# A decoder kernel on one core: a memory layer's centred values made by GpSimd in place of TensorE, with another order of work

## What is computed

```python
x = _layernorm(x + _L1_xattn_ref(x, ctx_1024, ctx_1024, ...), axis=-1)
...
Ctilde = jnp.einsum('bhid,bhjd->bhij', qh, kh) * D / TAU
maxit = jnp.maximum(jnp.abs(jnp.sum(Ctilde, axis=-1, keepdims=True)), jnp.exp(-max_d))
Htilde = jnp.einsum('bhij,bhjd->bhid', Ctilde, vh) / (maxit + 1e-06)
...
mean = jnp.mean(x, axis=-1, keepdims=True)
var = jnp.var(x, axis=-1, keepdims=True)
xn = (x - mean) / jnp.sqrt(var + 1e-05)
```

## Time and profile before

| what | value |
|---|---|
| median of three runs | 808.02 us (807.7 to 809.53) |
| profiled execution, span from first to last instruction | 808.1 us |
| its own time outside the span | not given by the page |
| PE busy | 738.1 us (91%) |
| PE weight loads busy | 485.7 us (60%) |
| DVE busy | 560.4 us (69%) |
| ACT busy | 347.2 us (43%) |
| POOL busy | 166.7 us (21%) |
| mean granted TensorE clock | 0.976 of full |

### The profile page before, as it was taken

The page is one execution under the profiler, slowest core; times in us unless marked ns, Lnnn a source line. Parts: engine busy times, 40 slices in busy tenths (PEclk is TensorE's granted clock), DMA queues, the critical chain, the costliest instruction groups (busy, mean ns, idle before and its releaser), DMA issues.

```text
span 808.1 us, 14850 instructions
## 1 busy us (share of the span) xinstructions
PE 738.1 (91%) x5976; PEld 485.7 (60%) x5976; DVE 560.4 (69%) x1405; ACT 347.2 (43%) x640; POOL 166.7 (21%) x249
## 2 busy tenths in 40 slices
PE   9999999989999978689979999999999998978494
PEld 6776565667657745557744576867656676646242
DVE  1558436575457589997899973647546569799887
ACT  3576223333144335565337634242324433485253
POOL 8711003010015030022330020011012513103300
PEclk9999999999999999999999999999999999988698
DMA  9402000000002000032000020000000000000001
GB/s 352 183 12 119 1 1 1 1 2 3 27 1 53 2 27 2 0 106 79 27 0 1 1 78 28 2 1 3 0 2 1 1 2 2 1 1 1 1 1 52
DMA packets 12739, 23.76 MB, mean 29 GB/s; under 512 B 768, under 2 KB 7040, under 8 KB 12416
## 3 DMA queue, kind: packets, MB, share of 16 engines
q1 hardware_dynamic: 12672, 22.82, 8.2%
HBM read 20.72 MB, written 2.10 MB: 28 GB/s over the span
## 4 chain that ended last, share of the span: by engine, by line
PE 73%; DVE 17%; ACT 4%; issue 2%; POOL 2%; DVEq 0%; ACTq 0%; POOLq 0%
PE bank L754 14%; PE bank L572 7%; PE bank L564 5%; PE bank L598 5%; PE bank L619 4%; PE bank L852 4%; PE bank L1104 3%; PE bank L764 3%; PE bank L740 3%; PE bank L833 2%; DVE work L1771 2%; PE bank L799 2%; PE bank L702 2%; PE bank L557 1%; PE bank L875 1%
## 5 line engine op out<-in xcount | busy, mean ns | idle before, releaser
L2160 POOL TENSOR_TENSOR rstd<-rstd,minus_half 128x2 f32<-128x2 f32 x56 | 43.1, 771 | 467.8 <-DVE rstd L1201 467.6
L754 PE MATMUL bank<-work,f0w 128*128 128x512 f16 x512 | 114.0, 379 | 0.0
L754 PEld LDWEIGHTS bank<-work,f0w 128*128 128x128 f16 x512 | 49.7, 98 | 59.5 <-issue 1.9
L1937 ACT ACTIVATE work<-bank 128x512 f16<-128x512 f32 x64 | 37.0, 596 | 83.7 <-PE bank L754 70.9
L1411 DVE SCALAR_TENSOR_TENSOR work<-bank,work 128x512 f16<-128x512 f32 x64 | 42.3, 685 | 35.3 <-ACT work L1937 35.2
L619 PE MATMUL bank<-work 128*128 128x256 f32 x208 | 50.2, 383 | 0.7 <-DVE work L1308 0.7
L1975 ACT ACTIVATE work<-bank 128x512 f32<-128x512 f32 x32 | 19.1, 596 | 72.6 <-PE bank L852 72.5
L1276 DVE TENSOR_REDUCE small<-bank 128x1 f32<-128x512 f32 (+3 forms) x32 | 18.8, 588 | 41.8 <-PE bank L600 41.7
L619 PEld LDWEIGHTS bank<-work 128*128 128x128 f32 x208 | 37.6, 190 | 6.8 <-issue 1.2
L1494 DVE TENSOR_TENSOR work<-bank,upper 128x512 f32<-128x512 f32 x32 | 22.0, 688 | 24.4 <-PE bank L852 24.3
L852 PE MATMUL bank<-work 64*128 64x128 f32 x512 | 37.2, 285 | 0.2 <-DVE work L1494 0.2
(11 more groups left out here) (307 smaller groups left out, 1698.1 us busy)
## 6 DMA issues: line engine op xcount, KB each, us to landing
work<-in_mask SPq DMA_DIRECT2D x4, 1024.0 KB, 7.0
xT<-in_xT SPq DMA_DIRECT2D x4, 512.0 KB, 4.0
ctxT<-in_ctxT SPq DMA_DIRECT2D x4, 512.0 KB, 4.7
perf_w<-in_k SPq DMA_DIRECT2D x3, 512.0 KB, 11.7
perf_w<-in_perf_w SPq DMA_DIRECT2D x1, 1536.0 KB, 6.2
x<-in_x SPq DMA_DIRECT2D x2, 512.0 KB, 11.7
ctx<-in_w SPq DMA_DIRECT2D x2, 512.0 KB, 13.8
work<-in_w SPq DMA_DIRECT2D x1, 1024.0 KB, 16.1
```

What stands on the lines that cost most here:

```text
L754: ins = nc.tensor.matmul(u.bank[:, :], f0w1[:, k, m * P:(m + 1) * P], s.h1[part][:, k, :], start=(k == 0 and part == 0), stop=(k == NF - 1 ...
L1937: nc.scalar.activation(dst[0][:, m, :], u.bank[:, :], ACT.Relu).then_inc(s.high_made.sem, 1)
L2160: nc.gpsimd.tensor_tensor(s.rstd[:, two], s.rstd[:, two], minus_half[:, 0:2], ALU.pow).then_inc(s.rstd_made.sem, 1)
```

## The change

The step mlstm.values goes from PE's and ACT's programs, and with it the matrix `centring`, its instruction on DVE, two bank uses per stream and round, and POOL's step mlstm.xT0. In its place POOL has a step mlstm.centre per stream and round, which reads the context in place, sums each head's 32 channels by halving adds in `s.l_v1`, scales by -1/32 and adds the mean to the context into `s.l_v1`. It stands in the front half: after the rstds of the cross step in round 1, after those of the sign step in round 0. `s.l_v1` moves to the end of the work region, which attention, sign and performer don't use.

```diff
@@ stream
-        s.l_v1 = w.cut(NT, LH, LV1)
...
+        w.at = w.words - NT * LH * LV1
+        s.l_v1 = w.cut(NT, LH, LV1)
@@ tensor_engine, back_half
-                if p == 0:
-                    yield "mlstm.values"
-
-                    if n == 0:
-                        pe.wait_ge(*centring_made.at(0))
-                    for i in range(2):
-                        u = s.banks["mlstm", n, "values", i]
-                        pe.wait_ge(*u.free)
-                        for j in range(2):
-                            t = 2 * i + j
-                            for k in range(NC):
-                                ins = nc.tensor.matmul(u.bank[:, j * C + k * P:j * C + (k + 1) * P], s.ctxT[:, k, t * P:(t + 1) * P],
-                                                       centring[:, :], start=True, stop=True)
-                        ins.then_inc(u.filled, 1)
@@ tensor_engine, the steps mlstm.state and mlstm.outT
-                    pe.wait_ge(*s.memory_ones.at(n))
-                    for i in range(2):
-                        pe.wait_ge(*s.banks["mlstm", n, "values", i].read)
+                    pe.wait_ge(*s.values_centred.at(n))
@@ vector_engine, prep
-            nc.vector.scalar_tensor_tensor(out=centring[:, :].rearrange("p (h d) -> p h d", d=LD), in0=mlstm_block[:, :, 0:LD],
...
@@ scalar_engine, back_half
-            yield "mlstm.values"
-            act.wait_ge(*s.memory_ones.at(n))
-            for i in range(2):
-                u = s.banks["mlstm", n, "values", i]
-                act.wait_ge(*u.full)
-                nc.scalar.copy(s.l_v1[:, 2 * i:2 * i + 2, :, 0:LD].rearrange("p t h d -> p (t h) d"),
-                               u.bank[:, :].rearrange("p (g d) -> p g d", d=LD)).then_inc(u.emptied, 1)
@@ gpsimd_engine
+        def centre(s, n):
+
+            yield "mlstm.centre"
+            pool.wait_ge(*s.ctx_in.all(n))
+            means, by_head = s.den2, ctx_of(s, n)[:, :, :].rearrange("p t (h d) -> p (t h) d", d=LD)
+            values = s.l_v1[:, :, :, :].rearrange("p t h d -> p (t h) d")
+            nc.gpsimd.memset(values[:, :, LD:LV1], 1.0)
+            half, src = LD // 2, by_head
+            while half >= 1:
+                out = values if half > 1 else means.unsqueeze(2)
+                m = gps.mark(nc.gpsimd.tensor_tensor(out[:, :, 0:half], src[:, :, 0:half], src[:, :, half:2 * half], ALU.add))
+                pool.wait_ge(*m)
+                half, src = half // 2, out
+            m = gps.mark(nc.gpsimd.tensor_scalar(means, means, -1.0 / LD, None, ALU.mult))
+            pool.wait_ge(*m)
+            nc.gpsimd.tensor_tensor(values[:, :, 0:LD], by_head,
+                                    means.unsqueeze(2).broadcast_to([P, NT * LH, LD]), ALU.add).then_inc(s.values_centred.sem, 1)
+
@@ gpsimd_engine, front_half
+            if n > 0:
+                yield from centre(s, n)
             for p in range(2):
                 yield from rstd(s, n, 3, p, "sign.")
+            if n == 0:
+                yield from centre(s, n)
@@ gpsimd_engine, back_half
-            yield "mlstm.xT0"
-            for p in range(2):
-                pool.wait_ge(*s.banks["perf", n, "out", p].full)
-            nc.gpsimd.memset(s.l_v1[:, :, :, LD:LV1], 1.0).then_inc(s.memory_ones.sem, 1)
```

More of the change, by code:

```diff
@@ L37 @@
     "tensor":
[8 rows of a table removed]
-    "vector":
[10 rows of a table removed]
-    "scalar":
[7 rows of a table removed]
[8 rows of a table added]
+    "vector":
[11 rows of a table added]
+    "scalar":
[7 rows of a table added]
     "gpsimd":
-        "a7 b2 a5 b5 a5 b2 a1 b3 a4 b1 a1 b4 a2 b1 a2 b1 a1 b2 a2 b1 a2 b1 a4 b2 a1 b2 a1 b5 a4 b4 w1 b1 a1 b1 a5 b10 a2 "
-        "b2",
+        "a7 b2 a2 b1 a3 b3 a1 b1 a5 b3 a4 b2 a1 b3 a1 b1 a1 b2 a2 b3 a1 b1 a4 b1 a2 b1 a1 b1 a1 b1 a1 b1 a1 b1 a1 b5 "
+        "a2 b1 a1 b1 a1 b2 w1 b1 a4 b1 a1 b9 a2 b2",
     "sync":
-        "w1 a2 w1 a1 w3 b1 w2 b1 a1 b1 w1 b1 a5 b1 a1 b1 a1 b6 a2 b1",
+        "w2 a1 w3 b1 a1 w1 b2 a1 b1 a1 w2 b1 a7 b7 a2 b1",
 }
 KEEP = {
[8 rows of a table removed]
[11 rows of a table added]
 }
@@ L236, in build @@
     mlstm_block = sb("mlstm_block", [P, LHT, LV1])
-    centring = sb("centring", [P, P])
     memory_back = sb("memory_back", [P, LHT, LV1])
@@ L361, in stream @@
         s.used, s.den_inverse = signal("masked_scores_used", NC * 2), signal("denominators_inverted", NC)
-        s.memory_ones, s.gate_low, s.softplus_made = (signal(name, 1) for name in ("memory_ones", "log_gate_in", "softplus"))
+        s.values_centred, s.gate_low, s.softplus_made = (signal(name, 1) for name in ("values_centred", "log_gate_in", "softplus"))
         s.key_gates, s.gates_final = (signal(name, 1) for name in ("key_gates_negated", "largest_gates_negated"))
@@ L397, in build @@
     head_rows_made, parts_made = Signal(sem("head_rows_made"), 1), Signal(sem("parts_made"), 1)
-    centring_made, taps_made = Signal(sem("centring_made"), 1), Signal(sem("taps_made"), 1)
+    taps_made = Signal(sem("taps_made"), 1)
     memory_back_made = Signal(sem("memory_back_made"), 1)
@@ L487, in plan_back @@
         s.banks.use(("mlstm", n, "xT", 0))
-        for i in range(2):
-            s.banks.use(("mlstm", n, "values", i))
         s.banks.use(("mlstm", n, "xT", 1))
@@ L1232, in prep @@
                                     ALU.mult).then_inc(sign_scale_made.sem, 1)
-            dve.wait_ge(constants_by_gpsimd, 1)
-            nc.vector.scalar_tensor_tensor(out=centring[:, :].rearrange("p (h d) -> p h d", d=LD), in0=mlstm_block[:, :, 0:LD],
-                                           scalar=-float(LD) ** -0.5, in1=ident[:, :].rearrange("p (h d) -> p h d", d=LD),
-                                           op0=ALU.mult, op1=ALU.add).then_inc(centring_made.sem, 1)
             for k in range(NC):
```

## The result

The changed kernel takes **818.85 us** (median of four runs, 815.75 to 822.01) beside 808.62 for the kernel before: ratio 1.0124, 95% interval 1.0104 to 1.0144. The prediction was 802.2 and its range ended at 811. The four runs stand in two pairs, 815.8 with a mean granted clock of 0.959 and 822.0 with 0.951; the profiled one is of the second pair (span 820.8), which is 12.7 us above.

What follows compares the result with a forecast made beforehand. PE was taken to bound the kernel, except at 300 to 350 and 700 to 760 us, where DVE sets the pace. Terms -4.6 + 0.9 + 0.8 - 3.5 + 0.5 = -5.9 from 808.1 gave 802.2 us, range 794 to 811.

Steps and rivals of the forecast that it cites:

- terms 4 and 5: The changed constant matmuls (+0.9 for their own time, +0.8 for the clock at the end) and the new order (-3.5).
- The values matmuls, -4.6: Four groups on PE removed: 1.79 us each at first and third, 0 at second, 1.0 at fourth; bounds 3.6 and 7.2.
- ACT and DVE relieved, 0: ACT loses two bank copies per group, DVE the matrix instruction; nobody waited for the copies until the state step, so 0.
- The centring, hidden: POOL centres the context, 6.7 us a group, 27 in all, within free gaps of its queue: 0 on the path.
- Constants, +1.7: Constant matmuls 80 to 71: 0.9 us for 12 more before the end, 0.8 for a falling clock at the end.
- The order, -3.5: a's first-round quantisation put ahead covers 4.5 us of PE waits, less 1.0 not made good; bounds -13.2 and +12.5.
- Ports, +0.5: DVE instructions slowed beside POOL's centrings, mainly a's second, where DVE is full: 0.5 us, between 0 and 6.7.
- Rival S: PE waits 12.5 us before a's quant.turn0 in round 0 and nothing comes back: 813.7 us; chance 0.15.
- Rival L: Port exclusion costs DVE all of a's second centring, 6.7 us in place of 0.5: 808.4 us; chance 0.07.
- DVE busy grows by over 5 us beside the centrings: A sign named in advance that the forecast is wrong: DVE's busy time up over 5 us beside POOL's centrings.
- the wait before quant.turn0: A sign of being wrong: PE waits over 8 us before a's quant.turn0 and the span is not shorter.
- Rival G: The order halves PE's idle time in 300 to 350 us, -10 in place of -3.5: 795.7 us; chance 0.18.

Runs made afterwards that it cites:

- e1: Kernel before with the new kernel's order tables and table of constant matmuls, values still by matmuls: 819.6 us, ratio 1.0125.
- e8: The new kernel unchanged, run again for times and a second profile: 818.8 us, ratio 1.0117.
- e14: New code in the old order, context loaded in time, POOL's centring between shift and weighing, no added constant matmuls: 808.8 us, ratio 1.001.
- e9: New code in the old order, context loaded in time, POOL waiting for DVE's shift and normalised tile before each centring: 810.8 us, ratio 1.0025.
- e7: New kernel with b's first centring behind a's two pow steps and two rstds on POOL: 816.5 us, ratio 1.0088.
- e2: New code with the old order tables and constant matmuls, POOL centring where it set the ones: 818.1 us, ratio 1.0108.
- e4: Kernel before with only the new table of constant matmuls: 817.1 us, ratio 1.0101.
- e3: New kernel with only the old table of constant matmuls: 820.6 us, ratio 1.0133.
- e11: New kernel with prep steps moved back at the start, e7's POOL order and e9's wait: 816.2 us, ratio 1.0091.
- e17: Old order, POOL centring after first.rstd and DVE's tile in three groups, before weighing in b's first, 8 constant matmuls added: 807.2 us, ratio 0.9993.
- e12: e11 with more constant matmuls, 113 in all: 811.7 us, ratio 1.0031.

## Why the prediction was wrong

The step that failed is the price of the new order with its constant matmuls, -1.8 us in terms 4 and 5; e1 measures +10.4. What the terms left out is PE's clock in the short waits that the new order and table leave: PE's work at the low level goes from 24.6 to 45.8 us there, and half of the difference, by the estimate above, is 10.6. The working took "0.9, as most stand at head and performer steps that wait" for the constants' own time, gave the order only the waits that it covers, and had a falling clock nowhere but at the end. By term:

1. **The values matmuls, -4.6.** This held, and was rather too small. In the new order the four groups bring 7.0 us (e1 against e8), the second 1.97 where I had 0. In the old order groups 1 and 3 bring 1.79 and 1.78, and groups 2 and 4 nothing (e14, e9): 3.6, my lower bound.
2. **ACT and DVE relieved, 0.** ACT is 3.0 us less busy and nobody gains by it.
3. **The centring, hidden.** 5.9 to 6.5 us a group for my 6.7, POOL +21.1 for +27. It was hidden at a's first. At b's first the 23 us gap of the earlier trace rows had been read in the old order, while the new one puts a's pows 15 us earlier: it is in front of them and 2.6 us on the path (e8 beside e1; gone in e7). At b's second the stretched DVE shift costs 0.8. The context was in place in the new order as worked out; e2 shows the 9.6 us that this wait costs where SP's order is not changed too.
4. **Constants, +1.7.** The end was 1.1 to 1.5 for my 0.8. The rest is the largest mis-sized term: I priced the others, 58 that become 70, by their own 0.216 us only, and looked for a falling clock only at the end. The table alone costs 7.9 us in the old order (e4).
5. **The order, -3.5.** The gaps that I read closed, by more than I said. The term failed in what it did not read: the first 25 us (DVE's and ACT's first steps behind a transfer), 250 to 300 (DVE crowded), the clock in the waits so opened. Order and constants together cost 10.4 us (e1, 819.6 less 809.2 on the same chip) where terms 4 and 5 have -1.8. How it divides between them depends on what is changed first: the table costs 7.9 in the old order (e4) and nothing clear in the new one (e3).
6. **Ports, +0.5.** DVE's instructions beside the four centrings, each against the median of its form, are stretched by 0, 2.6, 1.15 and 1.14 us, 4.9 in all, inside my 0 to 6.7 and ten times the value taken.

Rival S gave 813.7, the nearest figure, by a wait that is not there: L1069 waits 2.0 us for DVE in all four groups together. Rival L named the right mechanism at the wrong place and was too small to decide. "DVE busy grows by over 5 us beside the centrings" did not come about (4.9), "the wait before quant.turn0" neither. Rival G halves the 13.2 us of the first place and takes 10 for it, where half is 6.6. The error lay outside the signs that I had set.

**What stays open.** The mends don't add up (e11), and the time of one kernel follows its clock: 815.8 at 0.959 and 822.0 at 0.951 for the new one, 806.5 to 807.3 at 0.977 to 0.979 and 812.5 to 812.7 at 0.967 to 0.971 in e17. A rough estimate puts the new kernel near the prediction if its clock had held as before: half of the 33.6 us more at the low level is 16.8, and 820.8 less 16.8 is 804 (814.5 less 11.6 is 802.9 for e8). e12 goes there (profile at 806.4), but no version reaches it as a median, so this is argued and not shown. What remains of e12's 2.4 us was not separated. Why the clock falls at one wait and not at another like it is open too; no run here fixes where it falls.

## What to carry to other kernels

When an order changes, read the stretches where the bounding engine was full as closely as its gaps: a gap can only close, a full stretch can only open. Where a change brings less than counted, time the stretch around it between two marks, in several versions: here the removed work looked like a filler at two places, and the marks of later runs gave the loss to POOL's queue and to a locked-out instruction. Price a new order with the clock in mind: by the estimate for e8, what the new waits cost through it (11.6 us) is more than their own length (4.0). A step moved to a slack engine takes its input's transfer, its place in that engine's queue and the port with it, and each has to be looked up in the new order.

## What was not expected of the hardware

**The same work at either clock level, by the run.** The new kernel's two profiles, the first and then e8 4 us earlier, have the same steps here:

```profile
688.00:692.00 4.00, 3.62 (x49) 3.37 (x53) 2.52 (x11) 1.47 (x3) 1.36 (x11) 0.57 0.00 0
```
```profile
684.00:688.00 4.00, 4.00 (x76) 3.23 (x78) 3.28 (x13) 1.57 (x3) 1.25 (x10) 1.00 0.02 4
```
The first is 1.6 us further behind after it. Around 668 us e17 and the kernel before run the same steps after the same waits (e17 first):

```profile
664.00:668.00 4.00, 2.31 (x20) 0.96 (x13) 3.74 (x12) 2.35 (x5) 2.91 (x1) 1.00 0.00 0
668.00:682.00 14.00, 11.76 (x85) 9.69 (x90) 9.14 (x26) 2.25 (x5) 3.61 (x2) 0.51 0.00 1
```
```profile
664.00:668.00 4.00, 2.22 (x18) 1.24 (x21) 3.74 (x11) 2.09 (x4) 2.64 (x1) 1.00 0.02 4
668.00:682.00 14.00, 11.66 (x183) 8.48 (x181) 12.68 (x38) 3.85 (x8) 4.65 (x7) 1.00 0.01 1
```
e17 had been 1.1 us ahead and is 2.7 behind after it, 4.2 by 704 us; these 5.3 us are about as much as its two groups of runs lie apart (5.6). By the Trainium skill ("TensorE: Matmul & The Clock Gate", Part 1) the monitor runs free of the kernel, so that one kernel can meet it at another phase from run to run. The traces agree in that the same steps meet both levels; they can't show the phase.

**A lockout as long as the other engine's instruction.** DVE's shift of two elements a partition took 1.29 us when POOL's add of 1.28 began with it, one of 16 elements 1.90 beside POOL's 1.91. By the Trainium skill ("SBUF — State Buffer", "Who interferes with whom") a DVE instruction with two SBUF inputs and a GpSimd one that reads SBUF lock each other out whole. The trace agrees: in these two cases DVE's few elements took as long as the POOL instruction that they met.
